# One-core cross-attention and quantised FFN block: the last head pair through VectorE's transposes and the DMA shuffle, and FFN scales, bias and differences on GpSimd

## What is computed

```python
# attention over the context, 16 heads, added to x
h = layernorm(x)
q_big = einsum(reshape(h @ Wq.T), w_kc_q)           # per head, 192 wide
kv = rope(ctx)                                      # (2, 512, 64)
scores = (q_big @ W_qr) . (kv @ W_kr)               # (2, 16, 256, 512)
ctx_c = softmax(scores) @ kv                        # (2, 16, 256, 64)
x = x + (ctx_c @ w_kc_kv per head) @ Wo.T
# FFN with a weight made of four bit planes
h = layernorm(x)
soft = sigmoid(pweight) - sigmoid(nweight)          # (256, 256, 4)
weight = einsum('oin,n->oi', soft, exps * sigmoid(mask_weight)) * scale
bias = round_to_15_levels(clip(einsum('on,n->o', pbias - nbias, bexps))) * biasscale
x = x + h @ weight.T + bias
```

## Time and profile before

| what | us |
|---|---|
| median of 3 runs | 135.15 |
| lowest and highest of them | 134.89, 135.85 |
| profiled execution, device time | 135.59 |
| its span in the profile | 133.8 |
| busy in the span: PE, DVE, POOL, ACT | 126.7, 105.1, 85.7, 75.8 |

### The profile page before, as it was taken

How to read it: one execution, slowest core, us unless ns; L and a number is a source line. 1 busy time by engine, 2 the same in 40 slices (tenths; PEclk the granted TensorE clock), 3 DMA queues, 4 the chain that set the end, 5 groups by cost and what they waited for, 6 DMA issues and landing times.

```text
span 133.8 us, 2694 instructions
## 1 busy us (share of the span) xinstructions
PE 126.7 (95%) x990; PEld 95.5 (71%) x990; DVE 105.1 (79%) x159; ACT 75.8 (57%) x196; POOL 85.7 (64%) x126
## 2 busy tenths in 40 slices
PE   6999889999969999999999999999999999999991
PEld 6877679567747868976876896697685696766770
DVE  0386834999999693996999699699969989994192
ACT  4144545669469383847549486983975764534110
POOL 6417966969989949387958959768495570006040
DMA  3999987999898899999999899889998980000004
GB/s 88 251 323 228 174 100 262 222 185 235 225 237 201 153 192 232 260 284 258 231 283 289 229 194 328 240 213 257 333 245 199 263 225 18 0 0 0 5 0 157
DMA packets 29133, 26.15 MB, mean 195 GB/s; under 512 B 17056, under 2 KB 20768, under 8 KB 29120
## 3 DMA queue, kind: packets, MB, share of 16 engines
q1 hardware_dynamic: 26992, 22.84, 68.1%
q0 software_dynamic: 1456, 2.77, 8.8%
q10 hardware_dynamic: 672, 0.36, 0.9%
HBM read 10.50 MB, written 0.52 MB: 82 GB/s over the span
## 4 chain that ended last, share of the span: by engine, by line
PE 71%; DVE 13%; ACT 12%; issue 1%; ACTq 0%
PE score L975 14%; PE ctxb L991 13%; ACT probs L453 8%; DVE neg_max L657 7%; PE foldb L911 4%; PE score L1171 4%; PE proj L1021 4%; PE score L817 3%; DVE turned L673 3%; PE proj L1001 3%; PE ctxb L946 3%; PE foldb L926 2%; PE ctxb L1021 2%; PE foldb L1021 2%; PE score L1196 2%
## 5 line engine op out<-in xcount | busy, mean ns | idle before, releaser
L453 ACT ACTIVATE probs<-score,neg_max 128x512 f32<-128x512 f32 x64 | 43.3, 688 | 27.4 <-DVE neg_max L657 27.4
L391 POOL TENSOR_SCALAR probs<-probs,row_inv 128x512 f32<-128x512 f32 x64 | 44.0, 738 | 21.8 <-DVE row_inv L663 21.8
L657 DVE TENSOR_REDUCE neg_max<-score 128x2 f32<-128x1024 f32 x32 | 37.5, 1212 | 10.3 <-PE score L975 10.3
L975 PE MATMUL score<-k_t,q_t 64*128 64x256 f32 x256 | 32.3, 388 | 1.5 <-ACT probs L453 1.4
L673 DVE STREAM_TRANSPOSE turned<-probs 128x1024 f32<-128x1024 f32 x28 | 33.0, 1216 | 0.0
L975 PEld LDWEIGHTS score<-k_t,q_t 64*128 64x128 f32 x256 | 23.8, 186 | 7.5 <-issue 2.8
L383 POOL DMA_DIRECT2D wo<-in_L_xattn_Wo_dram x32 | 28.1, 1020 | 0.0
L991 PE MATMUL ctxb<-spread,kv 128*64 128x256 f32 x192 | 22.0, 382 | 0.0
L991 PEld LDWEIGHTS ctxb<-spread,kv 128*64 128x64 f32 x192 | 13.2, 137 | 8.1 <-issue 2.0
L453 ACT ACTIVATION_READ_ACCUMULATOR probs<-score,neg_max 128x1 f32 x64 | 13.1, 204 | 0.0
L410 POOL TENSOR_TENSOR wq<-wq,b_rows 128x256 f32<-128x256 f32 x3 | 2.2, 727 | 13.6 <-DVE wq L777 13.6
(11 more groups left out here) (152 smaller groups left out, 171.6 us busy)
## 6 DMA issues: line engine op xcount, KB each, us to landing
spread<-turned SPq DMA_DIRECT2D x56, 256.0 KB, 5.4
wo<-in_L_xattn_Wo_dram POOLq DMA_DIRECT2D x32, 64.0 KB, 4.7
wq<-in_L_xattn_Wq_dram SPq DMA_DIRECT2D x1, 1280.0 KB, 12.2
bulk<-in_L_ffn_pweight_dram SPq DMA_DIRECT2D x2, 512.0 KB, 7.1
bulk<-in_L_ffn_nweight_dram SPq DMA_DIRECT2D x2, 512.0 KB, 6.7
bulk<-in_L_xattn_w_kc_q_dram SPq DMA_DIRECT2D x4, 192.0 KB, 7.9
wq<-in_L_xattn_Wq_dram SPq DMA_DIRECT2D x1, 512.0 KB, 7.8
wkv<-in_L_xattn_w_kc_kv_dram SPq DMA_DIRECT2D x1, 512.0 KB, 5.2
```

Of the source, the lines that this page charges most:

```text
L391: pool.tensor_scalar(p, p, row_inv[:, j:j + 1], 1.0, ALU.mult, ALU.mult).then_inc(norm_made, 1)
L453: act.activation(probs[:, j, :], score[u % 2][:, h, :], ACT.Exp, bias=neg_max[:, j:j + 1], accum_out=row_sum[:, j:j + 1]).then_inc(exp_mad ...
L657: dve.tensor_reduce(neg_max[:, j:j + 2], score[u % 2][:], axis=AX, op=ALU.max, negate=True)\
L975: product = pe.matmul(score[u % 2][:, h, half * S:half * S + S], q_t[rows, i % 2, b, tt * P:tt * P + P], k_t[rows, b, half * S:half * S + ...
```

## The change

- The last pair takes the way of the others: two more halves of DVE turns and eight more shuffle DMAs on SP. PE's transposes of probabilities, ACT's copies of them and SP's four moves of the values are gone, and the late contexts of pair 7 read `spread` like those of pair 6.
- A key identity, permuted once by POOL (`key_ident`), lets the key transposes read it as it lies.
- POOL makes the scales (behind the first half of pair 5), the bias (first half of pair 6) and the two differences (behind the second half of pair 4, the fifth, and of pair 6). The tanh of the first weight half moves from pair 5 to pair 4.
- POOL's loads of Wo are placed earlier: pair 2 issues those of 3 and 4, pairs 3 to 5 those of 5 to 7, pair 6 none.
- DVE makes the first three bit planes of weight half 0 ahead of pair 6's maxima (`first_bits`), the fourth plane, the statistics and the mean between the turns of the last pair (`last_bits`), and weight half 1 behind the last turns.
- On PE the bias products and projections come first, then both late contexts of pair 6, their projections, and those of pair 7, batch by batch; the projections of pair 6 no longer wait for pair 7. The transposes of rows 0 and 1 stand behind the last late contexts.

```diff
-        kv_turned = ctx_rows
-        probs_t = turned[LASTP % 2][:].rearrange("p g j l r -> p (g j l r)")\
-            .rearrange("p (b l h s) -> p b l h s", b=B, l=LT, h=2)
         ctx_t = sb("ctx_t", [P, T * P])
...
-        trans_bank = [fold_bank[:], early[:, 0, :], early[:, 1, :], ctx_bank[:],
-                      fold_bank[:], early[:, 0, :], early[:, 1, :], ctx_bank[:]]
-        late_ctx_bank = [[late[:, 0, :], fold_bank[:]], [late[:, 1, :], early[:, 0, :]]]
+        late_ctx_bank = [[late[:, 0, :], late[:, 1, :]], [early[:, 0, :], fold_bank[:]]]
...
-            for i in range(LASTP):
+            for i in range(NP):
                 for half in range(2):
                     spread_probs(i, half)
-                if i == 0:
-                    for b in range(B):
-                        sp.wait_ge(kv_made[b], 1)
-                    for k in range(G):
-                        sp.dma_start(kv_turned[k * BK:k * BK + BK, :, :], kv[k:P:G, :, 0:DC]).then_inc(kv_moved, 16)
...
+            pool.wait_ge(ident_made, 1)
+            pool.tensor_copy(key_ident[:].rearrange("p (k c) -> p k c", k=G),
+                             ident[:].rearrange("p (c k) -> p k c", k=G)).then_inc(key_ident_made, 1)
...
+            def weight_scales():
+                pool.wait_ge(mask_made, 1)
+                pool.wait_ge(ld_small, 16 * 7)
+                link(pool.tensor_scalar(bits[:, 3, :], mask_t[:], 0.5, 0.5, ALU.mult, ALU.add))
+                link(pool.tensor_tensor(bits[:, 3, :], bits[:, 3, :], bits[:, 0, :], ALU.mult))
+                pool.tensor_scalar(bits[:, 3, :], bits[:, 3, :], scales[:, 0:1], 0.5, ALU.mult, ALU.mult)\
+                    .then_inc(scales_made, 1)
+
+            def bias_values():
+                link(pool.tensor_tensor(pb[:], pb[:], nb[:], ALU.subtract))
+                for t in range(DT):
+                    last = pool.tensor_tensor(pb[:, t, :], pb[:, t, :], bits[:, 1, :], ALU.mult)
+                link(last)
+                link(pool.tensor_tensor(pb[:, :, 0:2], pb[:, :, 0:2], pb[:, :, 2:4], ALU.add))
+                link(pool.tensor_tensor(b_raw[:], pb[:, :, 0], pb[:, :, 1], ALU.add))
+                link(pool.tensor_scalar(b_raw[:], b_raw[:], -1.0, 1.0, ALU.max, ALU.min))
+                link(pool.tensor_scalar(b_raw[:], b_raw[:], LEVELS, ROUND, ALU.mult, ALU.add))
+                link(pool.tensor_scalar(b_raw[:], b_raw[:], -ROUND, 1.0 / LEVELS, ALU.add, ALU.mult))
+                pool.tensor_scalar(b_col[:], b_raw[:], scales[:, 1:2], 1.0, ALU.mult, ALU.mult).then_inc(bias_made, 1)
+
+            def ffn_difference(ot):
+                pool.wait_ge(tanh_made, 2 * ot + 2)
+                pool.tensor_tensor(pw[:, ot, :], pw[:, ot, :], nw[:, ot, :], ALU.subtract).then_inc(difference_made, 1)
+
             for i in range(NP):
                 for half in range(2):
                     normalise(2 * i + half)
                     for j in range(K // BK):
                         if i == 0:
                             load_wo(half, j)
-                        elif i < LASTP and j // 2 == half:
-                            load_wo(i + 1, j)
+                        elif i < SECOND and j // 2 == half:
+                            load_wo(i + 1 if i < 3 else i + 2, j)
+                            if i == 2:
+                                load_wo(4, j)
+                    if i == 4 and half == 1:
+                        ffn_difference(0)
+                    elif i == 5 and half == 0:
+                        weight_scales()
+                    elif i == SECOND and half == 0:
+                        bias_values()
+                    elif i == SECOND:
+                        ffn_difference(1)
...
-                if i in (5, 6):
-                    act.wait_ge(ld_ffn[i - 5], 32)
-                    weight_tanh(2 * (i - 5))
-                    weight_tanh(2 * (i - 5) + 1)
+                if i in (4, 6):
+                    act.wait_ge(ld_ffn[(i - 4) // 2], 32)
+                    weight_tanh(i - 4)
+                    weight_tanh(i - 3)
...
-            for j in range(TT * 2):
-                take_transposed(j)
             take_values(values_count(LASTP), SECOND, NP)
-            take_late_contexts(SECOND, 0, 1)
-            for j in range(TT * 2, TT * 2 + 2):
-                take_transposed(j)
-            take_late_contexts(LASTP, 0, 2)
-            for j in range(TT * 2 + 2, TILES):
-                take_transposed(j)
             act.wait_ge(bias_spread, 1)
             act.activation(b_rows[:], bias_bank[:, 0:D], ACT.Copy).then_inc(bias_taken, 1)
-            take_late_contexts(SECOND, 1, 3)
+            take_late_contexts(SECOND, 0, 1)
+            take_late_contexts(SECOND, 1, 2)
+            take_late_contexts(LASTP, 0, 3)
             act.wait_ge(ffn_w_transposed, 1)
             act.activation(w_ffn_t.rearrange("p t d -> p (t d)"), ffn_w_bank, ACT.Copy)\
                .then_inc(ffn_w_taken, 1)
-            take_hidden(0)
-            take_hidden(1)
             take_late_contexts(LASTP, 1, 4)
-            take_hidden(2)
-            take_hidden(3)
+            for t in range(T):
+                take_hidden(t)
...
+            def turn_two(v, n):
+
+                i, half, j = v // 2, v % 2, 4 * (v % 2) + 2 * n
+                if i >= 2 and n == 0:
+                    dve.wait_ge(probs_spread[i % 2][half], landed(i - 2))
+                dve.wait_ge(norm_made, 4 * v + 2 * n + 2)
+                dve.transpose(turned[i % 2][:, :, j:j + 2, :, :].rearrange("p k j l r -> p (j l) k r"),
+                              probs[:, j:j + 2, :].rearrange("p j n -> p (j n)")).then_inc(probs_turned, 1)
...
+            def first_bits(ot):
+
+                dve.wait_ge(difference_made, ot + 1)
+                dve.wait_ge(scales_made, 1)
                 w_bits = pw[:, ot, :].rearrange("o (i n) -> o i n", n=NB)
                 link(dve.tensor_scalar(w_ffn[:, ot, :], w_bits[:, :, 0], bits[:, 3, 0:1], None, ALU.mult))
-                for n in range(1, NB):
-                    last = dve.scalar_tensor_tensor(w_ffn[:, ot, :], w_bits[:, :, n], bits[:, 3, n:n + 1],
-                                                    w_ffn[:, ot, :], ALU.mult, ALU.add)
-                    link(last)
+                for n in (1, 2):
+                    link(dve.scalar_tensor_tensor(w_ffn[:, ot, :], w_bits[:, :, n], bits[:, 3, n:n + 1],
+                                                  w_ffn[:, ot, :], ALU.mult, ALU.add))
+
+            def last_bits(ot):
+
+                w_bits = pw[:, ot, :].rearrange("o (i n) -> o i n", n=NB)
+                link(dve.scalar_tensor_tensor(w_ffn[:, ot, :], w_bits[:, :, 3], bits[:, 3, 3:4],
+                                              w_ffn[:, ot, :], ALU.mult, ALU.add))
                 link(dve.bn_stats(w_stats[:, ot, :], w_ffn[:, ot, :]))
                 link(dve.bn_aggr(w_mean[:, ot, :], w_stats[:, ot, :]))
...
+                if i == SECOND:
+                    first_bits(0)
...
-            ffn_difference(0)
+            turn_two(v, 0)
             inverses(v + 1)
-            ffn_scales()
-            ffn_weights(0)
-            ffn_difference(1)
-            ffn_weights(1)
+            turn_two(v, 1)
+            last_bits(0)
+            turn_probs(v + 1)
...
+            first_bits(1)
+            last_bits(1)
...
-                                        ident[:].rearrange("p (c k) -> p k c", k=G))
+                                        key_ident[:])
...
+            def late_contexts(i, b):
+                pe.wait_ge(probs_spread[i % 2][b], landed(i))
+                if i == SECOND:
+                    pe.wait_ge(exp_made, TILES * NP)
+                elif b == 1:
                     pe.wait_ge(fold_taken, values_count(LASTP))
...
                 for lt in range(LT):
                     for h in range(2):
...
+                        last = pe.matmul(late_ctx_bank[i - SECOND][b][64 * h:64 * h + 64, 0:S],
+                                         kv[:, b * LT + lt, h * DC:h * DC + DC], spread_columns(i, b, h, lt),
                                          start=(lt == 0), stop=(lt == LT - 1))
                 last.then_inc(late_made, 1)
 
...
+            def late_project(i, b):
+                pe.wait_ge(late_taken, 2 * (i - SECOND) + b + 1)
+                if i == SECOND and b == 1:
                     pe.wait_ge(early_added, 1)
...
                     pe.wait_ge(bias_taken, 1)
...
+                project(i, b, late_ctx[i - SECOND])
...
             values_side(LASTP)
...
+            pe.wait_ge(exp_made, TILES * LASTP + 6)
             pe.wait_ge(bias_made, 1)
             for ot in range(DT):
                 last = pe.matmul(bias_bank[:, ot * P:ot * P + P], b_col[:, ot:ot + 1].broadcast_to([P, P]),
                                  ident[:], start=True, stop=True)
             last.then_inc(bias_spread, 1)
...
+            projections(LASTP - 2)
+            late_contexts(SECOND, 0)
             late_contexts(SECOND, 1)
```

(78 more changed lines are left out.)

39 lines of the change are left out of this document (3 added, 36 removed).

## The result

| | before | changed |
|---|---|---|
| median of 14 runs each, us | 135.47 | 134.45 |
| lowest, highest | 134.89, 139.89 | 133.74, 135.88 |
| ratio, 95% interval | | 0.9929 [0.9906, 0.9951] |
| profiled execution, its span | 135.59, 133.8 | 133.74, 131.9 |

What follows compares the result with a forecast made beforehand. PE was taken to bound loop and tail. Last contexts at 121.1 plus 6.0 and 5.4 gave 132.5, less 0.8 for the keys 131.7 against 133.8 (-2.1): median 133.1 us, range 131.4 to 135.6.

Steps and rivals of the forecast that it cites:

- Last pair, shuffle and PE's new tail: Tail: last half turned at 114.6, landed 6.4 later at 121.0; last contexts from 121.1, then 6.0 and 5.4 us.
- Rival C: Last pair's shuffle goes as in the loop, last half ending 10.3 us behind its turn: +1.7, 136.9; chance 0.08.
- GpSimd's new work: POOL in the loop: difference 2.0 to 2.5 us, scales 0.9, bias 2.7, the bias hidden up to 5.4.
- Start of pair 6's maxima: VectorE in the loop: first bits ahead of these maxima move their start from 86.10 to 88.0.
- First and last bits beside the scaling: VectorE waits for GpSimd's scaling: one wait of 0.7 us at first bits, two of 0.3 to 0.4 at last bits.
- Key transposes: PE's two groups of key transposes with the plain identity: 0.35 + 0.45 = 0.8 us off everything behind; bounds 0 and 1.1.
- Tanh: ACT's two tanh move from pair 5 to pair 4, PE's 0.52 idle with them: net 0, bounds -0.3 and +0.5.
- From the profile to the median: Profiled execution lies 0.44 above the median, so 133.5 profiled should mean a median of 133.1.
- Rival B: Small waits eat the gain (bias 6.4 us, first bits 2.0, landing 8.0): gain 0 to 0.5, about 134.9; chance 0.19.

Runs made afterwards that it cites:

- e3: Changed kernel with the last bits of weight half 0 behind the last half's turns instead of ahead of them; 134.63 us, 0.9931 of the kernel before.
- e5: Changed kernel with all of VectorE's FFN weight bits, first and last, behind the last turns; 133.40 us, 0.9822 of the kernel before.
- e8: Changed kernel with all weight bits behind the last turns and the tanh behind ACT's copies; 133.07 us, 0.9792 of the kernel before.
- e11: e8 with w_kc_q's last part loaded ahead of Wq's last part on SP; 132.86 us, 0.9726 of the kernel before.
- e7: Changed kernel with GpSimd's three scale instructions ahead of the two Wo loads in pair 5; 133.57 us, 0.9834 of the kernel before.
- e4: Kernel before with the plain key identity alone; 135.42 us, 0.9979 of the kernel before.
- e2: Changed kernel with the last pair's eight shuffle DMAs moving one of four tiles (64 KB instead of 256); 133.39 us, 0.9811 of the kernel before.
- e9: e8 with four of the last pair's eight shuffle DMAs issued by ACT, four by SP; 132.98 us, 0.9737 of the kernel before.
- e10: e8 with the last pair's shuffle in 16 DMAs of 128 KB, four behind each turn; 133.28 us, 0.9770 of the kernel before.

## Why the prediction was wrong

By its own terms, the forecast was -0.8 for the keys, +0.7 for the loop (contexts of pair 5 at 104.0 instead of 103.31) and -2.0 for the tail: -2.1. The runs gave -0.4, +1.36 and, over the four profiles with this order of turns and shuffle (27.98, 29.00, 28.53 and 28.26), -2.05: -1.1, beside the median's 1.02. (The start ahead of the first mark varies by 0.9 and is left out.) So 0.7 of what is missing was lost in the loop and 0.4 at the keys.

- **Last pair, shuffle and PE's new tail: right in the sum, partly by luck.** 11.4 us from the last contexts to the end were forecast, 11.0 came. The last turn was forecast at 113.8 (114.6 less 0.8) and came at 113.65. But against pair 5's mark, which came later than forecast, the turn is 0.9 early (9.7 us behind it instead of 10.6), and the half then took 7.2 and 8.2 from its turn instead of 6.4: two errors of about a microsecond that cancel. What was wrong in it is the picture of one half behind its turn: e3, e5, e8 and e11 turn it 1.4 us sooner and it lands 17.3 to 18.4 behind the mark, no earlier than the 16.9 to 18.0 of the others. Rival C, the shuffle in the loop's manner, would have been 10.3.
- **GpSimd's new work: the step that failed.** I checked the bias against its gap and it fits (nine instructions, 95.26 to 97.7), as forecast. The first difference and the scales I priced (2.0 to 2.5 and 0.9) and then gave nothing, with no check of what stands beside them; the only room that I named there is the 2.4 us that POOL has free in a body, an average, and I named it for the Wo loads. In the stretch from 73 to 85 us there are a difference (2.4 of the chain), the Wo loads and the scales between scalings, and the free time was gone: first bits waited 0.56 for the scales. e7, which only takes the scales ahead of the loads, shows that this and what follows from it is 1.0 of the 1.36 us; the 0.36 left is less than the 0.7 that I had given for the whole delay. e5, without any first bits in the loop, gets back 1.26.
- **Start of pair 6's maxima: a slip in the sum.** 86.10 + 0.65 + 0.7 is 87.4, not the 88.0 that I went on with. They came at 87.81, which is 88.6 on the clock of the profile before: 0.5 from the tanh moved a body forward, 0.55 from the wait, 1.4 from the bits themselves.
- **First and last bits beside the scaling: right.** 0.79 instead of 0.44, 1.82 instead of 1.40, 0.80 instead of 0.69, 0.61 instead of 0.35: 1.14 in all, where 1.4 was forecast. The Trainium skill's rule ("SBUF — State Buffer", Who interferes with whom) agrees with these rows in which instructions pay: a multiply-add with two inputs in SBUF does, and the statistics between them, with one input, take 0.43 beside the scaling and 0.43 alone. In size it agrees less: the prediction has a block for a whole instruction, and in the changed kernel none of these lost more than 0.35, where one of the scaling takes 0.69. And `tensor_scalar`, with one input besides its scalars, pays too (0.79 and 0.61), which the rule as the prediction tells it doesn't cover.
- **Key transposes: mis-sized by half.** The chain's pieces shrank as read (0.92 and 1.05 to 0.49 and 0.59), but a shorter piece isn't a shorter chain: ACT's copy stood just behind the first, and PE's pieces behind both grew (e4). 0.37 came instead of 0.8, and in six of the twelve profiles a load stands in the chain and takes some of that back.
- **Tanh: right.** The 0.5 moved one pair earlier.
- **From the profile to the median: wrong.** I took a constant 0.44 between them. With a DMA in the chain's end, one execution's landing is a draw: 16.9 to 18.0 us behind the mark in four profiles of one order, and e2 spreads as much without it.

Rival B, many small waits that eat the gain, is closest to what happened, though not by the bias that it named. Its own terms don't add up to its price: S would be 123.5 to 124.2 and the end 134.1 to 134.8, a loss of 0.3 to 1.0 and not a gain of 0 to 0.5.

## What to carry to other kernels

Check the cover of each moved instruction in the very gap where it goes, with all that stands before it in that engine's queue; a body's average free time is no cover, and a small result that another engine waits for goes ahead of the loads. Work that nobody needs until the tail (here the weight bits) belongs behind the turns that release a transfer, since the loop had no room for it and the tail had, if only just: in e5, e9 and e10 it was then the FFN weight that PE waited for. Where a transfer becomes the last link, profile the kernel more than once before a span is compared.

## What the runs showed of the hardware that was not expected

- Eight shuffle DMAs of 256 KB issued with little else going took 11.5 to 13.0 us from the first issue to the last landing, 2 MB at some 160 to 180 GB/s, where the loop moves 248 at a DMA share of 0.96. The share was 0.76 between 109 and 121 us. An earlier turn (e3, e5, e8, e11) didn't bring the last landing forward; a second queue (e9) has it 0.9 earlier than e8 and 0.2 earlier than the best with one queue, within what executions differ by. With a quarter of the bytes (e2) half 0 lands 4.0 us after its first issue instead of 7.3 to 8.0, and no issue is held over 0.61, so most of the time above those 4.0 goes with the amount moved and not with the number of DMAs. What holds the rate wasn't found.
- GpSimd's `tensor_scalar` on 128x4 took 0.96 us in the changed kernel and 0.52 in e7, its like on 128x2 0.19 to 0.24. Both long records start before the instruction ahead of them has ended: in the changed kernel's chain the piece is 0.26.
- A strided read of the identity makes four transposes on PE take 0.92 to 1.05 us against 0.44 to 0.59 (matmuls of 409 against 272 ns each).
